# Halves of q made over 128 partitions and moved by DMA, in a pre-norm attention and mixture-of-experts layer

## The chip, the cores and the metric

The kernel runs on 1 core of one Trainium2 chip. The metric is the device time of one execution in microseconds; lower is better.

## The reference

The input x has 4 batches of 512 tokens of width 128. The layer adds an attention block, then a mixture of experts. Cut to what matters:

```python
def attention(x, ln1_g, ln1_b, Wq, Wkv, Wo, ln2_g, ln2_b):     # 16 heads of 64
    xn = layernorm(x, ln1_g, ln1_b)
    q = (xn @ Wq) * 64 ** -0.5                   # one q for each head
    k, v = split(xn @ Wkv)                       # one k and one v for all heads
    attn = softmax(einsum('bhid,bjd->bhij', q, k))
    out = einsum('bhij,bjd->bhid', attn, v)
    return layernorm(out @ Wo, ln2_g, ln2_b)

x = x + attention(layernorm(x), ...)
y = layernorm(x)
top 2 of 8 experts by softmax(y @ gate_w.T), weights scaled to sum 1
x = x + sum over the two of weight * (up * gelu(gate)) @ down
```

All is float32 in and out.

## The kernel before

**Precision.** TensorE multiplies float32 quickly in a format with a shorter mantissa. So q and k are kept as a high half (the value copied to that format) and a low half (the value less the high half). A head's q lies in `q_hl`: partitions 0 to 63 hold the high half, 64 to 127 the low half, so that one matmul over 128 partitions against `khh` (the high half of k, twice) adds high*high and low*high. `q_hm` holds the high half once more in partitions 0 to 63, and in partition 64 the negative row maximum of each query; a matmul with `kly` (low half of k and a row of ones) adds high*low and takes the maximum off. Both tensors have 10 slots, one for each head in turn.

**Steps.** `attention_schedule` makes one list of steps, sorted by a slot number and an order within it; every engine walks this list and does its part of each step, in that order. The unit is one score step: `EXP` n is at slot n, 256 in all (64 heads x 4 key tiles of 128), so 8 slots are a pair of heads and 64 slots a batch. What follows is measured in these slots.

- `Q` (line 1105 to 1107): TensorE makes q of a pair of heads in the bank `q_ps`, 128 partitions: 64 for each head.
- `QHI` (line 1077): ScalarE copies each head's 64 rows to the high half in `q_hl`, two instructions. `QLO` (line 1008): VectorE subtracts, two instructions, and writes partitions 64 to 127. GpSimd copies both high halves to `q_hm` (line 935).
- `MAX` (line 1170): TensorE computes high-part scores with queries on the partitions, 4 for each head; VectorE reduces them to row maxima (line 1019). Two buffers.
- `SHIFT` (line 1177): the maxima of four heads are turned; ScalarE writes them negated to `mrow` (line 1068); SP moves them by DMA to partition 64 of `q_hm` (line 871) and then issues four fills of the row lists in DRAM (line 877), as long as there are any.
- `EXP` (line 1199, 1201): the scores, keys on the partitions; ScalarE's exponential writes `prob` (line 1095).
- `PV` (line 1215): the product with v, TensorE. GpSimd adds up the probabilities (lines 950, 956). `SUM`, `RECIP`, `RSPLIT`, `NORM`, `OUT` normalize a unit of 8 heads and project them; `RSPLIT` writes `rhl` on VectorE (line 717), which `NORM`'s matmul (line 769) reads.
- Beside them run the layer norms, k and v of the next batch, and the routing of the batch before (`AFTER_STEPS`: `CHOOSE`, `RANK`, `PLACE` and so on, largely on VectorE; line 586 is the end of `CHOOSE5`; `RANK`'s matmuls are line 406 and behind), with GpSimd's indirect sends of rows (line 476).

The Q of pair k stands at slot 8k - 19 - lead (the lead is 6), the first MAX of the pair at 8k - 22, its first EXP at 8k. Pairs 0 to 3 have places of their own.

**The bank.** `q_ps` is shared by Q, k, v, the turned maxima and the routing: before TensorE writes it anew it waits for the reader of the last use (`bank_read`).

**SP.** The queue of DMAs that SP issues is in order. At step `V` of the last batch (slot 153) it issues the 8 loads of the experts' weights, 512 KB each (line 669), into `raw_w`, in front of the rows of `SHIFT` at slot 155, which TensorE waits for at slot 160.

Behind the attention a second block runs 39 tiles of 128 rows through the experts. SP loads each tile's rows; the last 22 are loaded into what was `psums`.

## Time and profile before

| | |
|---|---|
| median of 3 runs | 622.52 us (621.23 to 623.45) |
| span of the profiled execution | 619.0 us |
| TensorE busy | 576.5 us, 93% |
| VectorE busy | 419.2 us, 68% |
| GpSimd busy | 394.9 us, 64% |
| ScalarE busy | 303.0 us, 49% |
| DMA queue of SP | 24.50 MB, 12.1% of 16 engines' span |

The profile is of one execution. The span reaches from its first instruction to its last; the device time of a run has some microseconds around it, 3.5 by the median. The attention takes the span up to about 467 us, the experts the rest. An engine's share of busy time is an average over stages. The end of a matmul is modelled, so a busy TensorE can still wait inside a row; waits show as idle time in front of an instruction, with the instruction that ended it.

### The profile page before, as it was taken

To read this page: it belongs to the slowest core of one execution; us is meant where nothing else is said; L and a number is where in the kernel's file an instruction comes from. 1 tells how busy PE (TensorE), PEld (TensorE's weight loads), DVE (VectorE), ACT (ScalarE), POOL (GpSimd) and SP (SyncE) were. 2 spreads that over 40 slices of the span, in tenths; PEclk is the share of its full clock that TensorE was granted. 3 is DMA by queue.
4 is the path that set the end of the run, shared out by engine and by line. 5 is a ranking of instruction groups with operands and counts; after the bars stand their busy time and mean duration, and the time that the engine had idled before them with its cause. 6 is when DMAs were issued, how large, how long until landed. Compare 5 with 4: busy or idle time off the path is not lost. (4 is left out here: it accounts for less than half of the span.)

```text
span 619.0 us, 8823 instructions
## 1 busy us (share of the span) xinstructions
PE 576.5 (93%) x2611; PEld 328.8 (53%) x2611; DVE 419.2 (68%) x816; ACT 303.0 (49%) x568; POOL 394.9 (64%) x326
## 2 busy tenths in 40 slices
PE   8899999999999999989999988999998869999980
PEld 6455454454554454445544534444443558888870
DVE  4976659658747978875587789877487468444433
ACT  2345645355555554454656434455636453555530
POOL 5357667658668855698597558859746934454330
PEclk9999999999999999889999999999999999999995
DMA  6111011010101100070000000000006101230005
GB/s 177 69 70 70 25 48 69 1 69 6 65 28 43 71 1 2 4 272 32 2 0 2 1 2 18 18 1 1 9 2 191 46 22 32 66 92 27 26 11 203
DMA packets 23981, 29.29 MB, mean 47 GB/s; under 512 B 4403, under 2 KB 14901, under 8 KB 23936
## 3 DMA queue, kind: packets, MB, share of 16 engines
q1 hardware_dynamic: 21664, 24.50, 12.1%
q0 software_dynamic: 2272, 4.24, 2.0%
q8 instruction: 23, 0.38, 0.2%
q14 instruction: 22, 0.18, 0.1%
HBM read 13.73 MB, written 15.32 MB: 47 GB/s over the span
## 5 line engine op out<-in xcount | busy, mean ns | idle before, releaser
L1095 ACT ACTIVATE prob<-s_ps 128x512 f32<-128x512 f32 x256 | 150.5, 598 | 183.0 <-PE s_ps L1201 181.0
L1019 DVE TENSOR_REDUCE rowmax<-max_ps 128x1 f32<-128x512 f32 x256 | 173.1, 685 | 81.6 <-PE max_ps L1170 79.5
L950 POOL TENSOR_TENSOR fold<-prob 128x1024 f32<-128x1024 f32 x63 | 149.6, 2374 | 95.2 <-ACT prob L1095 94.7
L1215 PE MATMUL pv_ps<-prob,v 128*64 128x512 f32 x512 | 139.1, 623 | 0.0
L1199 PE MATMUL s_ps<-q_hl,khh 128*128 128x512 f32 x256 | 118.0, 461 | 0.6 <-ACT prob L1095 0.6
L1170 PE MATMUL max_ps<-khh,q_hl 128*128 128x512 f32 x256 | 103.6, 410 | 6.5 <-DVE q_hl L1008 3.3
L1201 PE MATMUL s_ps<-q_hm,kly 65*128 65x512 f32 x256 | 102.1, 399 | 0.0
L1199 PEld LDWEIGHTS s_ps<-q_hl,khh 128*128 128x128 f32 x256 | 48.6, 190 | 79.2 <-ACT prob L1095 59.8
L956 POOL TENSOR_TENSOR psums<-fold 128x512 f32<-128x512 f32 x63 | 81.7, 1296 | 4.9
L1170 PEld LDWEIGHTS max_ps<-khh,q_hl 128*128 128x128 f32 x256 | 49.1, 192 | 26.5 <-DVE rowmax L1019 9.4
L1201 PEld LDWEIGHTS s_ps<-q_hm,kly 65*128 65x128 f32 x256 | 48.8, 191 | 9.0 <-issue 3.4
L1215 PEld LDWEIGHTS pv_ps<-prob,v 128*64 128x64 f32 x512 | 25.7, 136 | 46.0 <-issue 35.1
L476 POOL DMA_INDIRECT sorted_rows<-xr,place_i x32 | 34.5, 1078 | 21.5 <-issue 12.2
L1008 DVE TENSOR_TENSOR q_hl<-q_ps,q_hl 64x512 fp32r<-64x512 f32 x64 | 44.1, 689 | 5.5 <-ACT q_hl L1077 4.2
L1550 PE MATMUL sum_ps<-wd,ht 128*128 x312 | 41.8, 277 | 6.0 <-DVE raw L1409 5.2
L1400 DVE TENSOR_TENSOR ha<-up_ps,gl 128x512 f32<-128x512 f32 x39 | 26.9, 691 | 29.5 <-PE up_ps L1528 22.8
L1550 PEld LDWEIGHTS sum_ps<-wd,ht 128*128 128x128 f32 x312 | 37.9, 192 | 7.4 <-issue 7.4
L1077 ACT ACTIVATE q_hl<-q_ps 64x512 fp32r<-64x512 f32 x64 | 37.6, 588 | 7.9 <-PE q_ps L1107 7.0
L1361 POOL DMA_INDIRECT parts<-raw,psums x22 | 21.3, 970 | 30.4 <-DVE raw L1409 27.6
L935 POOL TENSOR_SCALAR q_hm<-q_hl 64x1024 fp32r<-64x1024 f32 x32 | 33.3, 1040 | 6.7 <-ACT q_hl L1077 6.7
L727 DVE TENSOR_TENSOR ao<-sum_ps,raw 128x512 f32<-128x512 f32 x32 | 22.0, 689 | 21.6 <-PE sum_ps L769 21.3
L779 PE MATMUL y_ps<-ao,wof 128*128 128x512 f32 x64 | 34.8, 628 | 0.0
(227 smaller groups left out, 783.2 us busy)
## 6 DMA issues: line engine op xcount, KB each, us to landing
sorted_rows<-raw_w SPq DMA_DIRECT2D x36, 260.0 KB, 2.6
raw_w<-in_gate_upT SPq DMA_DIRECT2D x8, 512.0 KB, 7.5
wd<-in_downT SPq DMA_DIRECT2D x8, 256.0 KB, 3.6
raw_w<-parts SPq DMA_DIRECT2D x8, 256.0 KB, 4.6
psums<-sorted_rows SPq DMA_DIRECT2D x22, 65.0 KB, 1.8
x<-in_x SPq DMA_DIRECT2D x4, 256.0 KB, 5.8
out<-x SPq DMA_DIRECT2D x4, 256.0 KB, 2.5
xs_first<-sorted_rows SPq DMA_DIRECT2D x15, 65.0 KB, 2.2
```

The source lines that it names most:

```text
L779: nc.tensor.matmul(y_ps[:, :], wof[:, c, :], ao[:, k % 2, :], start=c == 0, stop=c == PAIRS - 1).then_inc(out_mm, 1)
L950: nc.gpsimd.tensor_tensor(fold[:, :, :], prob[:, head % 4, 0:2, :], prob[:, head % 4, 2:4, :], ALU.add).then_inc(prob_folded, 1)
L956: nc.gpsimd.tensor_tensor(psums[:, head % SUM_SLOTS, :], fold[:, 0, :], fold[:, 1, :], ALU.add).then_inc(head_sum, 1)
L1008: nc.vector.tensor_tensor(q_hl[DH:P, h % Q_SLOTS, :], q_ps[DH * hd:DH * hd + DH, :], q_hl[0:DH, h % Q_SLOTS, :].bitcast(F32), ALU.subtract ...
L1019: nc.vector.tensor_reduce(rowmax[:, group % 2, it, i:i + 1], max_ps[:, k % 2, :], AX_X, ALU.max).then_inc(max_done, 1)
L1077: nc.scalar.activation(q_hl[0:DH, (2 * k + hd) % Q_SLOTS, :], q_ps[DH * hd:DH * hd + DH, :], ACT.Copy).then_inc(q_hi, 1)
L1095: nc.scalar.activation(prob[:, head % 4, jt, :], s_ps[:, k % 2, :], ACT.Exp, scale=SCALE).then_inc(exp_done, 1)
L1170: nc.tensor.matmul(max_ps[:, k % 2, :], q_hl[:, k // JT % Q_SLOTS, it * P:(it + 1) * P], khh[:, b % 2, :], start=True, stop=True).then_inc ...
L1199: nc.tensor.matmul(s_ps[:, k % 2, :], khh[:, b % 2, keys], q_hl[:, slot, :], start=True, stop=False)
L1201: nc.tensor.matmul(s_ps[:, k % 2, :], kly[0:DH + 1, b % 2, keys], q_hm[0:DH + 1, slot, :], start=False, stop=True).then_inc(score_mm, 1)
L1215: last = nc.tensor.matmul(pv_ps[DH * hd:DH * hd + DH, :], v[:, b % 2, jt, :], prob[:, head % 4, jt, :], start=(jt == 0), stop=(jt == JT - 1))
L1550: last = nc.tensor.matmul(down_ps[:, :], ht[:, k % 2, c * P:(c + 1) * P], wd[:, weights(k, DN, c * P, P)], start=c == 0, stop=c == FC - 1)
```

## The change

For pairs 5 and up (`DIRECT = 5`), 27 of the 32:

- ScalarE makes the high halves of both heads by one instruction over 128 partitions into a new tile `qh`; VectorE the low halves by one into `ql`.
- A new step `QMOVE` on SP moves them by six DMAs of 64 partitions x 2 KB: the high half of each head to `q_hl`, the low half of each to `q_hl`, the high half of each to `q_hm`. GpSimd's copy is gone for these pairs. SP waits for `qh_made`, for the scores of the head that had the slot, and for `ql_made`.
- ScalarE and VectorE write `qh` and `ql` anew only when the moves of the pair before have landed. TensorE waits for the moves in place of the instructions.
- Q of these pairs stands at 8k - 27 - lead, 8 slots earlier; the Q of pair 5 at slot 13 (15 before).
- `mrow` has no tile of its own any more; it lies in partitions of `q_hm` that are otherwise unused. In the experts' block, the last 22 tiles share one semaphore for two loads each.

The diff, without the list of semaphore names:

```diff
@@ -61,11 +61,13 @@
     for pair in range(units * UP):
         u, p = divmod(pair, UP)
 
-        at = (-30, -11, *FIRST_Q_AT)[pair] if pair < 4 else 8 * pair - 19 - lead
+        at = (-30, -11, *FIRST_Q_AT)[pair] if pair < DIRECT + 1 else 8 * pair - 27 - lead
         place(at, 3, "Q", u, p)
         place(at + 1, 3, "QHI", u, p)
 
         place(-8 if pair == 1 else at + 1, 4, "QLO", u, p)
+        if pair >= DIRECT:
+            place(at + 1, 4.5, "QMOVE", u, p)
         for jt in range(JT):
             place(8 * pair + PV_AT[jt], 2, "PV", u, p * JT + jt)
         place(8 * pair + PV_AT[-1] + 1, 1, "RAW", u, p)
@@ -120,7 +122,9 @@
 LAST_STEPS = (("RECIP", 0), ("RECIP", 1), ("RECIP", 2), ("RECIP", 3), ("RSPLIT", 0), ("NORM", 0), ("NORM", 1), ("OUT", 0),
               ("NORM", 2), ("OUT", 1), ("NORM", 3), ("OUT", 2), ("OUT", 3))
 
-FIRST_Q_AT = (-3, 3)
+FIRST_Q_AT = (-3, 3, 7, 13)
+
+DIRECT = 5
 
 FIRST_SHIFT_AT = (-7.5, 2)
 
@@ -319,7 +323,15 @@
         tiles_ready = sem("tiles_ready")
         w_in = [sem(f"w_in{e}") for e in range(E)]
         down_mm = sem("down_mm")
-        xs_in = [sem(f"xs_in{k}") for k in range(NT)]
+        xs_in = [sem(f"xs_in{k}") for k in range(FIRST_TILES)] + [sem(f"xs_pair{n}") for n in range((REST + 1) // 2)]
+
+        def tile_in(k):
+
+            return k if k < FIRST_TILES else FIRST_TILES + (k - FIRST_TILES) // 2
+
+        def tiles_with(k):
+
+            return sum(tile_in(n) == tile_in(k) for n in range(NT))
         count = {"dve": 0, "pool": 0, "ln": 0, "ln_pool": 0, "ln_dve": 0}
 
         def link(dve, ins):
@@ -788,6 +800,8 @@
         with ExitStack() as att:
             q_hl = sb(att, "q_hl", [P, Q_SLOTS, S], F32R)
             q_hm = sb(att, "q_hm", [P, Q_SLOTS, S], F32R)
+            qh = sb(att, "qh", [P, S], F32R)
+            ql = sb(att, "ql", [P, S], F32R)
             xh = sb(att, "xh", [P, 2, S], F32R)
             xl = sb(att, "xl", [P, 2, S], F32R)
             wqh = sb(att, "wqh", [P, HEADS * DH], F32R)
@@ -805,7 +819,7 @@
             wvh = sb(att, "wvh", [P, DH], F32R)
             wvl = sb(att, "wvl", [P, DH], F32R)
             rowmax = sb(att, "rowmax", [P, 2, TPB, 4])
-            mrow = sb(att, "mrow", [4, 2, S], F32R)
+            mrow = q_hm[3 * P // 4:3 * P // 4 + 4, 0:2, :]
             prob = sb(att, "prob", [P, 4, JT, S])
             fold = sb(att, "fold", [P, 2, S])
 
@@ -824,6 +838,16 @@
 
             blank_set = sem("blank_set")
             mrow_in = [sem(f"mrow_in{n}") for n in range(2)]
+            q_in = sem("q_in")
+            qm_in = sem("qm_in")
+
+            def q_came(eng, k):
+
+                eng.wait_ge(q_in, 16 * 4 * (k - DIRECT + 1))
+
+            def q_top_came(eng, k):
+
+                eng.wait_ge(qm_in, 16 * 2 * (k - DIRECT + 1))
 
             def rows_came(eng, n):
 
@@ -859,6 +883,23 @@
                                  (gw[:, :], gate_wT), (tri[:, :, :], lower)):
                     sp.dma_start(dst, src).then_inc(consts2_in, 16)
                 for kind, u, a in steps:
+                    if kind == "QMOVE":
+                        k = u * UP + a
+                        parts_of = [slice(DH * hd, DH * hd + DH) for hd in range(2)]
+                        slots = [(2 * k + hd) % Q_SLOTS for hd in range(2)]
+                        sp.wait_ge(qh_made, k - DIRECT + 1)
+                        if 2 * k + 2 > Q_SLOTS:
+                            sp.wait_ge(score_mm, (2 * k + 2 - Q_SLOTS) * JT)
+                        for held, slot in zip(parts_of, slots):
+                            sp.dma_start(q_hl[0:DH, slot, :].bitcast(F32),
+                                         qh[held, :].bitcast(F32)).then_inc(q_in, 16)
+                        sp.wait_ge(ql_made, k - DIRECT + 1)
+                        for held, slot in zip(parts_of, slots):
+                            sp.dma_start(q_hl[DH:P, slot, :].bitcast(F32),
+                                         ql[held, :].bitcast(F32)).then_inc(q_in, 16)
+                        for held, slot in zip(parts_of, slots):
+                            sp.dma_start(q_hm[0:DH, slot, :].bitcast(F32),
+                                         qh[held, :].bitcast(F32)).then_inc(qm_in, 16)
                     if kind == "SHIFT":
                         head, heads = shift_heads[u]
 
@@ -927,7 +968,7 @@
                         for first, end in zip(WQ_PAIRS, WQ_PAIRS[1:]):
                             part = slice(first * P, end * P)
                             split(wq_raw[:, part], wqh[:, part], wql[:, part], wq_split)
-                    if kind == "Q":
+                    if kind == "Q" and u * UP + a < DIRECT:
                         k = u * UP + a
 
                         pool.wait_ge(q_hi, 2 * (k + 1))
@@ -1001,7 +1042,14 @@
                         nc.vector.tensor_tensor(kly[0:DH, b % 2, :], k_bank(b)[0:DH, :],
                                                 khh[0:DH, b % 2, :].bitcast(F32),
                                                 ALU.subtract).then_inc(kl_ready, 1)
-                    if kind == "QLO":
+                    if kind == "QLO" and u * UP + a >= DIRECT:
+                        k = u * UP + a
+                        dve.wait_ge(qh_made, k - DIRECT + 1)
+                        if k > DIRECT:
+                            q_came(dve, k - 1)
+                        nc.vector.tensor_tensor(ql[:, :], q_ps[:, :], qh[:, :].bitcast(F32),
+                                                ALU.subtract).then_inc(ql_made, 1)
+                    elif kind == "QLO":
                         for hd in range(2):
                             h = 2 * (u * UP + a) + hd
                             dve.wait_ge(q_hi, h + 1)
@@ -1067,12 +1115,16 @@
                             rows_came(act, u - 2)
                         nc.scalar.activation(mrow[0:heads, u % 2, :], shift_bank(u)[0:heads, :], ACT.Copy,
                                              scale=-1.0).then_inc(mrow_ready, 1)
-                    if kind == "QHI":
+                    if kind == "QHI" and u * UP + a >= DIRECT:
                         k = u * UP + a
                         act.wait_ge(q_mm, k + 1)
-                        if 2 * k >= Q_SLOTS:
-
-                            act.wait_ge(score_mm, (2 * k + 2 - Q_SLOTS) * JT)
+                        if k > DIRECT:
+                            q_came(act, k - 1)
+                            q_top_came(act, k - 1)
+                        nc.scalar.activation(qh[:, :], q_ps[:, :], ACT.Copy).then_inc(qh_made, 1)
+                    elif kind == "QHI":
+                        k = u * UP + a
+                        act.wait_ge(q_mm, k + 1)
                         for hd in range(2):
                             nc.scalar.activation(q_hl[0:DH, (2 * k + hd) % Q_SLOTS, :], q_ps[DH * hd:DH * hd + DH, :],
                                                  ACT.Copy).then_inc(q_hi, 1)
@@ -1111,7 +1163,8 @@
                     if kind in AFTER_STEPS:
                         return after_bank_read(kind, u)
                     return {"XT": (xnT_sb, u + 1), "K": (kl_ready, u + 1), "V": (v_ready, u + 1),
-                            "Q": (q_lo, 2 * (u * UP + a + 1)), "SHIFT": (mrow_ready, u + 1)}[kind]
+                            "Q": (q_lo, 2 * (u * UP + a + 1)) if u * UP + a < DIRECT else (ql_made, u * UP + a - DIRECT + 1),
+                            "SHIFT": (mrow_ready, u + 1)}[kind]
 
                 def keep_busy(times):
 
@@ -1160,8 +1213,10 @@
                     if kind == "MAX":
                         i, it = divmod(a, JT)
                         k = u * UH * JT + a
-                        if it == 0:
+                        if it == 0 and u * UH + i < 2 * DIRECT:
                             pe.wait_ge(q_lo, u * UH + i + 1)
+                        elif it == 0 and i % 2 == 0:
+                            q_came(pe, u * UP + i // 2)
                         if 2 <= k < 12:
                             keep_busy(BUSY["rows"])
                         if k >= 2:
@@ -1190,7 +1245,10 @@
                             n = first_heads.index(k // JT)
                             rows_came(pe, n)
                         if a % (2 * JT) == 0:
-                            pe.wait_ge(q_top, u * UP + i // 2 + 1)
+                            if u * UP + i // 2 < DIRECT:
+                                pe.wait_ge(q_top, u * UP + i // 2 + 1)
+                            else:
+                                q_top_came(pe, u * UP + i // 2)
                         if k >= 2:
 
                             pe.wait_ge(exp_done, k - 1)
@@ -1510,7 +1568,7 @@
                         pe.wait_ge(xeh_ready, k)
                     else:
                         pe.wait_ge(xel_ready, k - RAW_TILES)
-                    pe.wait_ge(xs_in[k], 16)
+                    pe.wait_ge(xs_in[tile_in(k)], 16 * tiles_with(k))
                     nc.tensor.transpose(xt_ps[:, :], rows(k)[:, 0:P], ident[:, :]).then_inc(xt_mm, 1)
 
                 def weights(k, of_each, first, width):
```

Where Q of pairs 5 and 6 goes on TensorE: the rows of slots 14 and 15, before and then after the change (`s_ps` are the two score matmuls of a slot, `max_ps` a MAX matmul).

```order
L1199 MATMUL s_ps<-q_hl,khh 128x512
L1201 MATMUL s_ps<-q_hm,kly 128x512
L1170 MATMUL max_ps<-khh,q_hl 128x512
L1215 MATMUL pv_ps<-prob,v 64x512 x2
L1199 MATMUL s_ps<-q_hl,khh 128x512
L1201 MATMUL s_ps<-q_hm,kly 128x512
L1170 MATMUL max_ps<-khh,q_hl 128x512
L1105 MATMUL q_ps<-xh,wqh 128x512
L1106 MATMUL q_ps<-xh,wql 128x512
L1107 MATMUL q_ps<-xl,wqh 128x512
```

```order
L1157 MATMUL q_ps<-xh,wqh 128x512
L1158 MATMUL q_ps<-xh,wql 128x512
L1159 MATMUL q_ps<-xl,wqh 128x512
L1257 MATMUL s_ps<-q_hl,khh 128x512
L1259 MATMUL s_ps<-q_hm,kly 128x512
L1225 MATMUL max_ps<-khh,q_hl 128x512
L1273 MATMUL pv_ps<-prob,v 64x512 x2
L1257 MATMUL s_ps<-q_hl,khh 128x512
L1259 MATMUL s_ps<-q_hm,kly 128x512
L1225 MATMUL max_ps<-khh,q_hl 128x512
L1157 MATMUL q_ps<-xh,wqh 128x512
L1158 MATMUL q_ps<-xh,wql 128x512
```

In both, the first score matmul shown is that of slot 14. Before, the first Q shown behind slot 15 is pair 5's; after, pair 5's stands in front of slot 14 and pair 6's is the one behind slot 15.

The same place on ScalarE, from the exponential of slot 13 on; `q_hl` rows are the two high halves of a pair, `qh` the new one. Before:

```order
L1095 ACTIVATE prob<-s_ps 128x512 x4
L1077 ACTIVATE q_hl<-q_ps 64x512 x2
L1095 ACTIVATE prob<-s_ps 128x512 x4
L737 ACTIVATE raw<-pv_ps 128x512
L1095 ACTIVATE prob<-s_ps 128x512 x2
L372 ACTIVATE x<-x,offset,rstd 128x128 x4
L1095 ACTIVATE prob<-s_ps 128x512 x2
L1077 ACTIVATE q_hl<-q_ps 64x512 x2
```

After:

```order
L1147 ACTIVATE prob<-s_ps 128x512 x2
L1124 ACTIVATE qh<-q_ps 128x512
L1147 ACTIVATE prob<-s_ps 128x512 x2
L1124 ACTIVATE qh<-q_ps 128x512
L1147 ACTIVATE prob<-s_ps 128x512 x4
L749 ACTIVATE raw<-pv_ps 128x512
L1147 ACTIVATE prob<-s_ps 128x512 x2
L384 ACTIVATE x<-x,offset,rstd 128x128 x4
```

Only two exponentials, those of slots 15 and 16, now stand between the high half of pair 5 and that of pair 6.

SP's queue around the loads of the weights, before: rows of the maxima (`mrow`), fills (`sorted_rows`), and the weight loads (`raw_w<-in_gate_upT`) behind the rows of slots 123 and 139.

```order
L871 DMA q_hm<-mrow 1x2x512 x2
L877 DMA sorted_rows<-raw_w 128x520 x4
L871 DMA q_hm<-mrow 1x2x512 x4
L669 DMA raw_w<-in_gate_upT 128x1024 x8
L871 DMA q_hm<-mrow 1x2x512 x12
```

After, from the moves of slot 152 on:

```order
L894 DMA q_hl<-qh 64x512 x2
L898 DMA q_hl<-ql 64x512 x2
L901 DMA q_hm<-qh 64x512 x2
L681 DMA raw_w<-in_gate_upT 128x1024 x8
L912 DMA q_hm<-q_hm 1x2x512 x2
L894 DMA q_hl<-qh 64x512 x2
```

The weight loads are issued behind the moves of slots 144 and 152, of which the second pair's wait for the Q of slot 151; the rows of slot 155 are still the next behind the loads.

## Rows read from the trace of the kernel before

**Rows 1.** The page: span, and TensorE's busy time, share and instructions.

```profile
span 619.0 us, 8823 instructions
PE 576.5 (93%) x2611; PEld 328.8 (53%) x2611; DVE 419.2 (68%) x816; ACT 303.0 (49%) x568; POOL 394.9 (64%) x326
```

**Rows 2.** The page's groups of instructions: count, busy us, mean ns, idle before.

```profile
L1095 ACT ACTIVATE prob<-s_ps 128x512 f32<-128x512 f32 x256 | 150.5, 598 | 183.0 <-PE s_ps L1201 181.0
...
L1008 DVE TENSOR_TENSOR q_hl<-q_ps,q_hl 64x512 fp32r<-64x512 f32 x64 | 44.1, 689 | 5.5 <-ACT q_hl L1077 4.2
...
L1400 DVE TENSOR_TENSOR ha<-up_ps,gl 128x512 f32<-128x512 f32 x39 | 26.9, 691 | 29.5 <-PE up_ps L1528 22.8
...
L1077 ACT ACTIVATE q_hl<-q_ps 64x512 fp32r<-64x512 f32 x64 | 37.6, 588 | 7.9 <-PE q_ps L1107 7.0
...
L935 POOL TENSOR_SCALAR q_hm<-q_hl 64x1024 fp32r<-64x1024 f32 x32 | 33.3, 1040 | 6.7 <-ACT q_hl L1077 6.7
```

**Rows 3.** Busy time, clock and DMA share in the stretch 78 to 450 us.

```profile
78.00:450.00 372.00, 362.68 (x1487) 178.64 (x1486) 272.89 (x484) 191.47 (x360) 269.98 (x196) 0.99 0.09 31
```

**Rows 4.** Line 1008, who waited for it: us in total, times.

```profile
  PE max_ps L1170: 3.3, 3
```

**Rows 5.** Timeline from 244 us: start, us, engine, line.

```profile
245.18 1.05 POOL L935 TENSOR_SCALAR q_hm<-q_hl 64x1024 fp32r<-64x1024 f32 x1
...
246.16 0.68 DVE L1019 TENSOR_REDUCE rowmax<-max_ps 128x1 f32<-128x512 f32 x1
246.87 1.41 DVE L1008 TENSOR_TENSOR q_hl<-q_ps,q_hl 64x512 fp32r<-64x512 f32 x2
...
247.61 0.75 PE L1170 MATMUL max_ps<-khh,q_hl 128*128 128x512 f32 x1 [1.56 <-DVE q_hl L1008]
...
249.79 1.71 PE L1215 MATMUL pv_ps<-prob,v 128*64 128x512 f32 x4
...
251.43 0.41 PE L406 MATMUL q_ps<-picked,before 128*128 128x32 f32 x2
```

**Rows 6.** Timeline from 360 us.

```profile
363.25 1.41 DVE L1008 TENSOR_TENSOR q_hl<-q_ps,q_hl 64x512 fp32r<-64x512 f32 x2
...
363.98 0.49 PE L1170 MATMUL max_ps<-khh,q_hl 128*128 128x512 f32 x1 [1.47 <-DVE q_hl L1008]
...
365.43 0.50 PE L1170 MATMUL max_ps<-khh,q_hl 128*128 128x512 f32 x1 [0.49 <-DVE rowmax L1019]
```

**Rows 7.** Two short stretches; the last three numbers are clock, DMA share, GB/s.

```profile
248.00:250.00 2.00, 2.00 (x6) 0.90 (x7) 1.68 (x4) 0.60 (x1) 0.07 (x1) 0.50 0.00 0
272.00:275.00 3.00, 3.00 (x8) 0.89 (x6) 1.88 (x4) 1.67 (x3) 2.68 (x3) 0.50 1.02 410
```

**Rows 8.** Timeline from 266 us.

```profile
270.05 0.50 PE L769 MATMUL sum_ps<-rhl,headsel 128*128 128x512 f32 x1 [2.10 <-DVE rhl L717]
```

**Rows 9.** Timeline: the first score matmul of slots 14 and 19.

```profile
50.92 0.41 PE L1199 MATMUL s_ps<-q_hl,khh 128*128 128x512 f32 x1
...
58.73 0.40 PE L1199 MATMUL s_ps<-q_hl,khh 128*128 128x512 f32 x1
```

**Rows 10.** The weight loads (line 669), then the timeline of slots 151 to 160.

```profile
L669 SPq DMA_DIRECT2D raw_w<-in_gate_upT x8: 424/432/710, 266.7 to 270.2; - x8
...
DMA to landing us min/median/max: 4.1/7.5/10.7
...
289.18 1.20 ACT L1077 ACTIVATE q_hl<-q_ps 64x512 fp32r<-64x512 f32 x2
...
298.90 1.19 SPq L871 DMA_DIRECT2D q_hm<-mrow  x2
...
304.09 0.40 PE L1199 MATMUL s_ps<-q_hl,khh 128*128 128x512 f32 x1
```

**Rows 11.** The page's DMA issues: count, KB each, median us to landing.

```profile
sorted_rows<-raw_w SPq DMA_DIRECT2D x36, 260.0 KB, 2.6
...
gw<-in_gate_wT SPq DMA_DIRECT2D x1, 4.0 KB, 4.4
```

6 lines of the change are left out of this document (3 added, 3 removed).

## Prediction

> **What bounds the kernel now.** I read the page first. TensorE is busy 93% of a span of 619.0 us [rows 1], and the change does not touch its work: the same 2003 rows of TensorE code are in both programs. So the change can only give back time in which TensorE waits, or take more. The table by stretches says how much there is. From 78 to 450 us, the steady part of the attention, TensorE is busy 362.68 of 372 us [rows 3]: at most 9.3 us are idle, and some of that belongs to waits the change does not touch. The totals on the page mislead here. ScalarE is busy half of the span, VectorE two thirds, and both wait for TensorE; taking work from an engine that waits gives nothing by itself.
>
> Then I asked who waits for the instruction that the change replaces, VectorE's low halves of q (line 1008). TensorE's MAX matmul waited for it 3 times, 3.3 us together [rows 4]. Two of these waits are long. I number the 256 score steps (EXP) as slots; a pair of heads is 8 slots.
>
> - At 247.61 a MAX matmul starts after 1.56 us idle [rows 5]. The reader is to see the row above it: VectorE came to the row maximum only at 246.16, behind the routing work of the batch before, and to the two q halves at 246.87. The MAX matmul stands for the first head of the pair whose halves are being made, so it waits for the first of them.
> - At 363.98 the same, 1.47 us, and at 365.43 another 0.49 us for the row maximum that the halves had delayed [rows 6]. This is the same place of the next batch.
>
> The first of these also costs clock: the granted clock is 0.50 in the stretch 248 to 250, that is 1.2 GHz instead of 2.4 [rows 7], after a gap of 1.56 us. The second gap, nearly as long, cost none.
>
> A third long wait, 2.10 us at 270.05, is for rhl [rows 8], not for q; it too is followed by a stretch at 0.50 [rows 7].
>
> **The change, part by part.** It holds for 27 of the 32 pairs.
>
> *ScalarE.* Two instructions of 588 ns become one over 128 partitions. The nearest row is the exponential of the same shape, 598 ns [rows 2]; so 27 x 0.58 = 15.7 us less. ScalarE waits for TensorE in this part, so: 0 on the path.
>
> *VectorE.* Two of 689 ns become one; VectorE's product of the same shape (line 1400) takes 691 ns [rows 2]. 27 x 0.69 = 18.6 us less. Where VectorE is behind, this matters; I count it inside the two places below and nowhere else.
>
> *GpSimd.* 27 copies of 1040 ns go away [rows 2], 28 us. GpSimd waits for ScalarE's probabilities in most of this time: 0. One of these copies, at 245.18 to 246.23, lies in front of the late row maximum at 246.16 [rows 5]; it may give up to 0.5 us there, which I don't count.
>
> *The longer lead.* From pair 6 on, Q stands 8 slots earlier, exactly one pair. So in the steady state each slot has the same instructions as before, made for the next pair. The first MAX of a pair comes 11 slots behind its Q instead of 3. The MAX matmul of 247.61 could start where TensorE went idle, 247.61 - 1.56 = 246.05. The next MAX then needs the row maximum that ends at 246.84, about 0.2 us of wait, and the PV group that started at 249.79 starts at about 247.2; the matmuls at 251.43 come at 248.2 [rows 5]: 3.2 us, of which about half is clock. At 363.98 the same working gives: MAX at 363.98 - 1.47 = 362.5, the next one at 363.3 (limited by the row maximum right ahead of the halves, which start at 363.25), so 365.43 becomes 363.3: 2.1 us [rows 6]. The third wait on q is the rest, under 0.3 us, and lies in the first pairs, which are unchanged. Sum of the gains: 5.3 us. Bounds: below, the 3.0 us of the two idle times alone; above, 3.2 + 2.1 plus 2 us if the lighter VectorE also shortens the wait at 270.05.
>
> *The moves.* Six DMAs a pair, 128 KB each, 162 in all. Issue: SP's DMAs of the maxima rows take 0.60 us each, the weight loads 0.50 [rows 10], so 3.0 to 3.6 us a pair. Landing: the 260 KB fills take 2.6 us [rows 11], an upper bound for half the bytes. At the 410 GB/s of [rows 7] 260 KB are 0.6 us of it; 2.0 stay as the way in and out, the lower bound, and with 0.3 for 128 KB I take 2.3. So a pair's q is in place about 6 us behind its high half, and the MAX that reads it comes 10 slots, some 17 us, later: hidden in the steady state. The DMA engines are busy 0.09 of this stretch [rows 3] and take 768 KB more each 13.9 us (slots 14 to 160 take 304.09 - 50.92 us [rows 9, 10], 1.73 a slot). If that cover were gone, each pair would wait up to 4 us.
>
> *The start.* Pair 5's Q goes to slot 13 and pair 6's to slot 15, two slots apart. Pair 6's high half on ScalarE waits until all moves of pair 5 have landed. Slot 14 starts at 50.92 [rows 9]; Q of pair 5 now stands in front of it and takes 0.7. High half done about 53.4, low half 54.4, last move issued at 56.0 to 56.4, landed at 58.3 to 58.8. Pair 6's high half is then done at 58.8 to 59.4 and the exponential of slot 17 behind it at 59.4 to 60.0. TensorE's slot 19, at 58.73 before [rows 9], would come at 59.7 (0.7 for the second Q, 0.3 for the bank) and needs that exponential: a wait of 0 to 0.4. With the bank and the row maximum queued behind the low half on VectorE I take 0.6 us lost; bounds 0.3, and 2.5 if the moves take twice as long. The 0.7 of the earlier Q comes back at the end.
>
> *The weight loads.* SP's queue is in order, and this is the one place that it is pushed. The 8 loads of the experts' weights were issued from 266.7, behind the rows of slot 139 [rows 10]. They stand at slot 153 in SP's list, and until now nothing held SP. Now the moves of slots 144 and 152 stand in front, and those of 152 wait for the low half of the Q of slot 151. That Q's high halves start at 289.18 [rows 10]; with one instruction the high half is done at 289.8, the low at 290.5, six issues end at about 293.1, and the loads follow, 26 us later than before. They took 270.2 + 10.7 - 266.7 = 14.2 us from first issue to last landing, with GpSimd's own sends between them; the 4.19 MB alone at the 410 GB/s of [rows 7] take 10.2, and with 2.0 for the way in and out 12.2. So they end at 305.3 (bounds 304.6 and 307.4). Behind them in the queue come the maxima rows of the next four heads, issued at 298.90, which TensorE needs at 304.09 [rows 10]. A DMA of 4 KB behind a full queue does wait: gw took 4.4 us to land behind the x loads [rows 11]. The rows so land at about 305.5: 1.4 us of wait, bounds 0.6 and 3.4. The clock decides what such a wait is worth beyond itself; I take nothing for it here and price it in rival 2.
>
> No row here shows a transfer over 64 partitions. The Trainium skill (SBUF — State Buffer, "Door 1: The DMA port swizzle") says that partitions 0 to 63 reach 8 of 16 ports, with 218 GB/s as the limit. By it, an estimate, a move takes 0.6 us of transfer instead of the 0.3 that 410 GB/s gives, the last moves reach 0.6 us further into the weight loads, and the sum would be 0.6 us higher. The sum goes by the rows.
>
> *The end.* Tiles from 17 on wait for two row loads instead of one. They run some tiles ahead of TensorE: 0.
>
> **Sum.** -5.3 + 0.6 + 1.4 = -3.3 us; the profile's 619.0 becomes 615.7. Around the span lie 622.52 - 619.0 = 3.5 us. Some of the 2 us of VectorE's relief and of the 0.5 us that GpSimd's missing copy may give are likely, so I forecast -3.7: 618.8 us. A difference under 0.3%, 1.9 us, can't be told from none.
>
> **Rivals.**
> 1. *The rows come in time.* If the loads end by 304, or the rows' two packets don't wait for the whole queue, only the start costs: -5.3 + 0.6 = -4.7, with the other relief up to -6.5: 616.0 to 617.8. Against it speaks the landing of gw. 0.15.
> 2. *The gain is eaten.* A gap of 1.56 us cost clock and one of 1.47 did not [rows 5 to 7]; the wait behind the weights is about as long. With it some 1.6 us more; and if the late row maxima take the place of the wait for q (DVE stays behind by the routing work), the gain falls to 3.0. Then -3.0 + 0.6 + 1.4 + 1.6 = +0.6, or with one of the two -1.7: 620.8 to 623.1, no change. 0.22.
> 3. *Slower: rows behind the weights.* The loads end at 307.4 or later because moves and loads share the engines; TensorE waits 3.4 us or more, falls to 1.2 GHz for 2 us, and the probabilities of the head behind come late: 6 or more against 5.3, with the start at its 2.5. +2.5 to +4: 625 to 626.5. It decides once wait and clock together pass 6.6 us (5.3 + 1.9 - 0.6). 0.13.
> 4. *The change does nothing*: the two waits stay, since they were VectorE's lateness. Against it, MAX at 247.61 starts at once with the end of the first q half, 0.74 us into the pair, and not with the row maximum. With it nothing is gained and the losses of 2.0 stay: 624.5; 0.02, counted in rival 3.
>
> My forecast, -1.9 to -5.0, has 0.50. Faster than 0.3%: 0.50 + 0.15 = 0.65; same 0.22; slower 0.13. The range leaves out the far part of rival 3 and little else: 615.0 to 623.3; the likeliest case alone holds 617.5 to 620.6.
>
> **What would show it.** Right: no wait of MAX for q at about 244 and 358; the granted clock 1.00 where it was 0.50 at 248; ScalarE idle some 2 us or more at about 56 for a DMA; a wait of TensorE for a DMA in front of the score matmul of slot 160, near 300 in the new span, with the weight loads issued at about 290; one VectorE operation of about 690 ns per pair. Wrong: that last wait missing or over 3 us, MAX waiting for the row maximum at the two places, or moves that take over 4 us to land.

## The result, and the profile after

The changed kernel takes 625.38 us (median; 622.66 to 628.13), the kernel before on the same chip 622.28 us (617.94 to 626.67). The ratio is 1.006, 95% interval 1.0036 to 1.0083: slower, by more than 0.3%. I had forecast 618.8 us and given this side 0.13. Measured again, the same kernel gave 1.0074 (below). Ratios, here and below, are of fast runs alone (a few slow or stray ones are left out of them), and so they are not quite the quotients of the medians.

The page of the changed kernel, top and groups:

```profile
span 625.0 us, 8929 instructions
...
PE 580.8 (93%) x2611; PEld 331.1 (53%) x2611; DVE 398.8 (64%) x789; ACT 288.3 (46%) x541; POOL 367.7 (59%) x299
...
L1257 PE MATMUL s_ps<-q_hl,khh 128*128 128x512 f32 x256 | 118.7, 464 | 3.7 <-DMA q_hm<-q_hm 2.1
L1225 PE MATMUL max_ps<-khh,q_hl 128*128 128x512 f32 x256 | 103.8, 411 | 5.8 <-DVE rowmax L1067 4.3
...
q_hm<-qh SPq DMA_DIRECT2D x54, 128.0 KB, 2.3
```

VectorE, ScalarE and GpSimd have 20, 15 and 27 us less to do than in [rows 1], as they should, and a move lands in 2.3 us, as forecast. None of this bounds the kernel. The span is 6.0 us longer all the same, and TensorE is busy 4.3 us more (576.5 in [rows 1]) with the same 2611 matmuls: a good part of the loss is not idle time but matmuls at the lower clock. The lines to read are still the idle times of TensorE, since the clock falls behind them: the score matmul of line 1257 waited 2.1 us for a DMA, and MAX (line 1225) 4.3 us for row maxima.

The two profiles are not equally lucky. In every run on record the device time is 1.7 to 2.1 us above the run's span, and not the 3.5 us that I had put there. So the profile before, of 619.0 us, is of an execution of about 620.8 us (an estimate from these), about 1.5 under the median of 622.28. That of the changed kernel took 626.78 us, 1.4 over its median. About half of the 6.0 us is this choice.

To find the places I took from both traces the start of the first score matmul of every pair (of 8 slots), and of tiles of the experts' block, and subtracted. Pairs are counted from 0; "again" is experiment 11, "four edits" experiment 12, and the last column experiment 9. Each number is what is lost (+) or won (-) between one mark and the next, in us, profile against profile:

```
                               changed kernel     four edits    kernel before, list step
                               first   again      to it         one slot earlier
pair 0 -> 1                     +0.03   +0.16     -1.42          -0.18
pair 1 -> 3 (Q of 5 and 6)      +2.22   +2.17     +0.66           0.00
pair 3 -> 16                    +0.01    0.00      0.00          -0.01
pair 16 -> 19                   -2.15   -3.76     -3.76          -1.52
pair 19 -> 21 (slot 160)        +2.37   +4.83      0.00           0.00
pair 24 -> 26                   -2.63   -2.66     -2.68          +4.47
pair 26 -> 27                   +3.85   +5.32     -0.02           0.00
pair 27 -> 28 (Q of 5 returned) -1.00   -1.01     -1.00          -0.01
tile 0 -> 8                     +2.34   +1.26     +1.39          +2.18
tile 17 -> 20                   +0.83   +0.71      0.00          +0.03
```

The -1.42 at pair 0 -> 1 is no gain of the edits: the kernel of experiment 3 has it too, with a granted clock of 1.00 from 12 to 50 us where the kernel before has 0.96. Tile 8 -> 17 was 0.2 us longer in the first column and 2.0, 2.0 and 2.7 us in the others; everything else is under 0.9 us. Three of my steps are seen at their places: the start, slot 160, and the two late row-maximum places (pairs 16 and 24). Two losses I had not priced: pair 26, and tile 17.

**The start.** Timeline of the changed kernel, from the first to the second new Q:

```profile
52.26 0.59 ACT L1124 ACTIVATE qh<-q_ps 128x512 fp32r<-128x512 f32 x1
...
55.55 1.24 SPq L901 DMA_DIRECT2D q_hm<-qh  x2
...
58.89 0.60 ACT L1124 ACTIVATE qh<-q_ps 128x512 fp32r<-128x512 f32 x1 [3.09 <-DMA q_hm<-qh]
59.39 1.08 ACT L1147 ACTIVATE prob<-s_ps 128x512 f32<-128x512 f32 x2
...
59.52 0.69 DVE L1050 TENSOR_TENSOR ql<-q_ps,qh 128x512 fp32r<-128x512 f32 x1 [3.39 <-ACT qh L1124]
60.03 0.50 PE L1257 MATMUL s_ps<-q_hl,khh 128*128 128x512 f32 x1 [0.82 <-ACT prob L1147]
```

The second `qh` waits 3.09 us for the moves of the first. Behind it stands an exponential, and TensorE waits 0.82 us for that, so slot 19 starts at 60.03 (58.73 in [rows 9]). A MAX matmul behind it waits 0.54 us more for the row maximum that VectorE makes behind the late low half.

**Slot 160.** The weight loads, the rows of the maxima behind them, and the score matmul that needs these:

```profile
L681 SPq DMA_DIRECT2D raw_w<-in_gate_upT x8: 432/446/592, 293.1 to 296.7; - x8
...
DMA to landing us min/median/max: 3.6/6.9/9.7
...
298.52 1.29 SPq L912 DMA_DIRECT2D q_hm<-q_hm  x2
...
305.99 0.50 PE L1257 MATMUL s_ps<-q_hl,khh 128*128 128x512 f32 x1 [2.11 <-DMA q_hm<-q_hm]
```

The last load lands at 296.7 + 9.7 = 306.4. The rows, issued 1.8 us behind it, come only near the end of this stretch: TensorE is idle for 2.11 us, until 305.99.

**Pairs 16 and 24.** Where [rows 5] have two low halves in 1.41 us and MAX waiting 1.56 us for them, there is now:

```profile
247.34 0.68 DVE L1067 TENSOR_REDUCE rowmax<-max_ps 128x1 f32<-128x512 f32 x1
...
247.94 0.68 DVE L1050 TENSOR_TENSOR ql<-q_ps,qh 128x512 fp32r<-128x512 f32 x1
...
248.17 0.47 PE L1225 MATMUL max_ps<-khh,q_hl 128*128 128x512 f32 x1 [0.33 <-DMA q_hl<-qh]
...
249.27 0.50 PE L1225 MATMUL max_ps<-khh,q_hl 128*128 128x512 f32 x1 [0.18 <-DVE rowmax L1067]
```

The DMA that the first wait names belongs to the next pair; what ended here is the row maximum, at 248.02. The granted clock stays at 1.00, where [rows 7] have 0.50. At pair 24 it is the same with 0.27 and 0.18 us (1.47 and 0.49 in [rows 6]), and a part of the gain lies one pair further on, at a matmul that waits for `rhl`. First before, then after:

```profile
385.21 0.50 PE L769 MATMUL sum_ps<-rhl,headsel 128*128 128x512 f32 x1 [1.61 <-DVE rhl L717]
```

```profile
384.58 0.50 PE L781 MATMUL sum_ps<-rhl,headsel 128*128 128x512 f32 x1 [0.37 <-DVE rhl L729]
```

The wait of 2.10 us in [rows 8], for the same product, did not get shorter: it is 2.30 us.

**Pair 26**, the place that I had not looked at. First the kernel before, then the changed one, VectorE and GpSimd only:

```profile
391.03 1.05 POOL L935 TENSOR_SCALAR q_hm<-q_hl 64x1024 fp32r<-64x1024 f32 x1
...
392.25 1.07 POOL L476 DMA_INDIRECT sorted_rows<-xr,place_i  x1 [0.17 <-issue]
...
393.31 0.17 DVE L628 TENSOR_SCALAR taken<-more_upto 128x8 f32<-128x8 f32 x1
...
394.59 2.42 POOL L950 TENSOR_TENSOR fold<-prob 128x1024 f32<-128x1024 f32 x1
```

```profile
391.89 0.97 POOL L488 DMA_INDIRECT sorted_rows<-xr,place_i  x1 [0.30 <-issue]
...
392.69 2.62 DVE L640 TENSOR_SCALAR taken<-more_upto 128x8 f32<-128x8 f32 x1
392.87 2.39 POOL L991 TENSOR_TENSOR fold<-prob 128x1024 f32<-128x1024 f32 x1
...
395.34 1.29 POOL L997 TENSOR_TENSOR psums<-fold 128x512 f32<-128x512 f32 x1
395.54 1.12 DVE L643 TENSOR_TENSOR more_upto<-more_upto,more 128x8 f32<-128x8 f32 x1
396.69 0.69 DVE L1067 TENSOR_REDUCE rowmax<-max_ps 128x1 f32<-128x512 f32 x1
...
397.44 0.80 PE L1225 MATMUL max_ps<-khh,q_hl 128*128 128x512 f32 x1 [2.04 <-DVE rowmax L1067]
```

Line 628 is now line 640: an operation on 128x8 elements of the routing's list step. It took 0.17 us, and takes 2.62, ending when GpSimd's `fold` beside it ends. Before, the fold started 1.28 us behind this operation, and now 0.18 us; the difference is the copy of 1.05 us that stood in GpSimd's queue in front of two sends and the fold, with nothing between them but the sends' issue (0.17 and 0.30 us). The row maximum queued behind it comes late, MAX waits 2.04 us, and the granted clock falls to 0.50 in 398 to 400.

### The profile page after: what moved, and what is told of

Read it like the earlier page. It is cut to its first block and busy times, and to the rows that moved or that the text cites. A ratio compares the mean times of both kernels' runs of the same rounds, so it can differ in the third digit from the quotient of the medians.

```text
span 625.0 us, 8929 instructions
## 1 busy us (share of the span) xinstructions
PE 580.8 (93%) x2611; PEld 331.1 (53%) x2611; DVE 398.8 (64%) x789; ACT 288.3 (46%) x541; POOL 367.7 (59%) x299
## 5 line engine op out<-in xcount | busy, mean ns | idle before, releaser
L1528 ACT ACTIVATE ht<-q_ps 128x512 f32<-128x512 f32 x39 | 23.3, 597 | 24.5 <-PE q_ps L1595 22.9
L1520 ACT ACTIVATE gl<-gate_ps 128x512 f32<-128x512 f32 x39 | 23.3, 598 | 19.1 <-PE gate_ps L1586 16.1
L720 DVE RECIPROCAL rinv<-sum_ps 128x128 f32<-128x128 f32 x32 | 29.9, 941 | 2.6 <-PEq L800 2.6
```

The costliest lines, as they stand in the source:

```text
L720: last = nc.vector.reciprocal(rinv[:, quarter], sum_ps[:, quarter])
```

## Experiments

All were timed beside the kernel before, whose median was 622.54 us beside 1 to 4, 620.57 beside 5 to 8 and 624.12 beside 9 to 12, each time on another chip. So kernels of different groups are compared by their ratios, and not by their medians. Ratios are to the kernel before, with the 95% interval.

**1. Weight loads first.** SP issues the eight loads right behind the maxima rows of slot 139, ahead of the moves of slots 144 and 152, and not at step `V`:

```diff
+                        if u == 10:
+                            sp.wait_ge(rows_filled, 16 * FILLS)
+                            for e in range(E):
+                                load_gate_up(sp, e)
-                    if kind == "V" and u == NB - 1:
-                        sp.wait_ge(rows_filled, 16 * FILLS)
-                        for e in range(E):
-                            load_gate_up(sp, e)
```

> The changed kernel with one part undone: SP issues the 8 weight loads where the kernel before did, right behind the rows of slot 139, ahead of the moves of slots 144 and 152. Theory (rows behind the weights): the wait of the score matmul of slot 160 for a DMA, 2.3 us in the changed kernel's profile, goes, pair 19 takes 16.1 us again instead of 18.3, and the time is some 2.3 us less than the changed kernel's 625.4. Rival (the queue only shifts the wait): the weights now delay the moves of slot 144, and the time stays within 1 us of 625.4.

622.18 us, ratio 1.0019 (0.9991 to 1.0047), span 620.2. The loads are issued from 265.4, the wait at slot 160 is gone (0.00 at pair 19 -> 20, +2.27 with the change alone). So this loss was the order in SP's queue. The ratio fell by 0.4%, about what I had expected (2.3 us).

**2. Q of pair 6 three slots later.** Slot 18 and not 15 (the condition that picks `FIRST_Q_AT` takes in one pair more, not shown):

```diff
-FIRST_Q_AT = (-3, 3, 7, 13)
+FIRST_Q_AT = (-3, 3, 7, 13, 18)
```

> The changed kernel with pair 6's Q at slot 18 in place of slot 15, so that Q of pairs 5, 6 and 7 stand 5 slots apart. Theory (ScalarE waits for the round trip of pair 5's moves): ScalarE's idle 3.1 us for a DMA in front of the second high half goes, and pairs 1 and 2 together lose their 1.5 us; the time is 1.5 us less than 625.4. Rival (the loss of pairs 1 and 2 is the extra Q in this stretch alone): nothing changes.

624.55 us, ratio 1.0031 (0.9995 to 1.0067). Pair 1 -> 3 costs 0.62 and not 2.22: the extra Q alone is left, 1.6 us are saved. In this profile the second high half no longer waits:

```profile
59.21 0.59 ACT L1124 ACTIVATE qh<-q_ps 128x512 fp32r<-128x512 f32 x1
...
59.83 0.69 DVE L1050 TENSOR_TENSOR ql<-q_ps,qh 128x512 fp32r<-128x512 f32 x1 [0.19 <-ACT qh L1124]
```

**3. The lead alone**, in the kernel before, without single instructions or moves:

```diff
-        at = (-30, -11, *FIRST_Q_AT)[pair] if pair < 4 else 8 * pair - 19 - lead
+        at = (-30, -11, *FIRST_Q_AT)[pair] if pair < 6 else 8 * pair - 27 - lead
-FIRST_Q_AT = (-3, 3)
+FIRST_Q_AT = (-3, 3, 7, 13)
```

> The kernel before with one part of the change alone: Q of pairs 5 and up 8 slots earlier, still with two instructions per half and GpSimd's copy, no moves. Theory (the lead is what gives time back, the moves only cost): both waits of MAX for q go, 2.5 us at pair 16 and about 2 at pairs 24 and 25, no wait at slot 160, no start loss: 617 to 619 us, some 4 us less than the kernel before. Rival (the lighter VectorE and GpSimd gave the gain): MAX waits for the row maximum at the same places and the time is within 1.5 us of 622.3.

626.44 us, ratio 1.0079 (1.0049 to 1.0109): slower. The wait for q is gone and two waits for row maxima stand in its place:

```profile
246.31 0.68 DVE L1019 TENSOR_REDUCE rowmax<-max_ps 128x1 f32<-128x512 f32 x1
247.01 1.41 DVE L1008 TENSOR_TENSOR q_hl<-q_ps,q_hl 64x512 fp32r<-64x512 f32 x2
247.13 0.47 PE L1170 MATMUL max_ps<-khh,q_hl 128*128 128x512 f32 x1 [0.91 <-DVE rowmax L1019]
...
249.20 0.80 PE L1170 MATMUL max_ps<-khh,q_hl 128*128 128x512 f32 x1 [1.13 <-DVE rowmax L1019]
```

My expectation of 617 to 619 us failed, and the gain that I put down to the lead is not the lead's. MAX waits 0.91 + 1.13 us here, about as much as the kernel before waits in the execution of experiment 4 (1.57 + 0.33), and at both places the two profiles lose the same against the profile before: 1.80 us at pair 16 -> 19 and 3.1 at pair 24 -> 26. In the times all twelve runs lie at 624.6 or above, while the kernel before reaches down to 618.0. It also loses at the start: pair 1 -> 3 costs 1.63 us without a single move, 0.69 of it a wait of TensorE for the bank, and 0.71 comes back at pair 27 -> 28.

In the changed kernel the two waits at pair 16 are 0.33 and 0.18 us. Experiment 8 tells which part of the change took away which.

**4. Row pairs alone.** The kernel before with one semaphore for the loads of two tiles, as in the diff.

> The kernel before with the semaphores of the last 22 row loads shared by two, as in the changed kernel, and nothing else. Theory (the first of these tiles waits for the second load and TensorE's sequencer gets to the next tile late): 0.8 to 1.1 us more than the kernel before, with TensorE idle about 0.5 to 0.8 us in front of the first gate matmul behind the turn of tile 17. Rival (the loads are ahead): no difference, and the 0.8 us in the changed kernel's profile come from elsewhere.

624.02 us, ratio 1.0018 (0.9979 to 1.0056). The time tells nothing; the profile has +0.89 at tile 17 -> 20, the same loss as in the changed kernel. Its attention is that of the kernel before, and yet it has +3.38 at pair 16 -> 17 and +3.15 at pair 24 -> 25 against the profile before. This is the clock. The rows below give the stretch and its length, then busy time and instructions of TensorE, its weight loads, VectorE, ScalarE and GpSimd, then granted clock, DMA share and GB/s. First the kernel before, then this one, in the stretches behind the wait for q:

```profile
250.00:252.00 2.00, 2.00 (x9) 0.66 (x8) 0.59 (x1) 0.00 (x0) 2.00 (x1) 0.72 0.00 0
252.00:254.00 2.00, 2.00 (x15) 1.09 (x14) 1.11 (x2) 1.35 (x3) 1.57 (x2) 1.00 0.00 0
```

```profile
250.00:252.00 2.00, 2.00 (x5) 0.39 (x6) 0.69 (x1) 0.00 (x0) 1.94 (x1) 0.50 0.00 0
...
254.00:256.00 2.00, 2.00 (x8) 0.90 (x11) 1.04 (x2) 1.63 (x3) 0.00 (x0) 0.50 0.00 0
256.00:258.00 2.00, 2.00 (x9) 0.50 (x2) 1.90 (x12) 0.00 (x0) 0.31 (x2) 0.50 0.00 0
```

The same matmuls after the same wait: the clock is back at 1.00 behind 252 in one execution and still at 0.50 in 256 to 258 in the other. So one profile of the kernel before is no fair base for the gain. Pair 16 -> 19 is 1.80 later here, and against this execution the change wins 3.9 to 5.6 us there instead of 2.2 to 3.8.

**5. Three repairs.** The changed kernel with 1 and 2 and a semaphore of its own for tile 17 (`tile_in` is shifted by one to fit, not shown):

```diff
-        xs_in = [sem(f"xs_in{k}") for k in range(FIRST_TILES)] + [sem(f"xs_pair{n}") for n in range((REST + 1) // 2)]
+        xs_in = [sem(f"xs_in{k}") for k in range(FIRST_TILES + 1)] + [sem(f"xs_pair{n}") for n in range(REST // 2)]
```

> The changed kernel with three parts undone at once: the weight loads back behind the rows of slot 139, pair 6's Q at slot 18, and the load of tile 17 on a semaphore of its own. Theory (the three losses are separate and add up): -2.3 or more at slot 160, -1.5 at pairs 1 and 2, -0.8 at tile 17, so 4 to 5 us less than the changed kernel's 625.4: about 621. The loss at pair 26 stays. Rival (they only moved the phase of the clock): the sum is under 3 us and other stretches give it back.

619.37 us, ratio 0.9984 (0.9951 to 1.0016), span 616.4: no difference to the kernel before that can be told. Slot 160 and tile 17 -> 20 are at 0.00, pair 26 -> 27 at +4.37, as expected.

**6. The list step one slot earlier.** The changed kernel with this alone:

```diff
-AFTER_AT = (29, 30, 33, 43, 51, 52, 54, 54, 55, 57, 58, 60, 63, 67, 69, 82, 84, 86, 88)
+AFTER_AT = (29, 30, 33, 43, 51, 52, 54, 54, 55, 57, 58, 60, 63, 67, 69, 81, 84, 86, 88)
```

> The changed kernel with VectorE's first list step of the batch (LIST0) one slot earlier, nothing else. In the changed kernel one VectorE instruction of this step, over 8 elements a partition, takes 2.62 us at 392.7 because GpSimd's send and its fold stand in the way, and MAX then waits 2.04 us for the row maximum, pair 26 taking 17.4 us instead of 13.6. Theory (a collision of VectorE with GpSimd that GpSimd's missing copy moved here): with the step elsewhere the 2.6 us instruction is short or costs under 1 us, and the time is 2 to 4 us less than 625.4. Rival (VectorE is simply behind here): the wait stays.

620.93 us, ratio 0.9989 (0.995 to 1.0028). Pair 26 -> 27 goes from +3.85 to -0.02. The operation takes its short time again, well ahead of the fold:

```profile
390.80 0.99 POOL L488 DMA_INDIRECT sorted_rows<-xr,place_i  x1 [0.15 <-POOL psums L997]
391.02 0.17 DVE L640 TENSOR_SCALAR taken<-more_upto 128x8 f32<-128x8 f32 x1
...
393.08 2.40 POOL L991 TENSOR_TENSOR fold<-prob 128x1024 f32<-128x1024 f32 x1
```

The operation lies inside one of GpSimd's sends here and is not held up, so a send alone does not hold it. In the changed kernel it started 0.17 us before a send ended and lasted through the fold.

**7. All four**, 5 and 6 together.

> The three parts of a_three and the earlier list step together. Theory: the four add up to 6 to 8 us less than the changed kernel: 617 to 619 us, below both kernels. Rival: phase effects of the clock eat half of it, 620 to 622.

615.21 us (613.33 to 617.17), ratio 0.9898 (0.9862 to 0.9934), span 611.9. Faster than both kernels, by more than I had expected (617 to 619; the kernel before was 1.7 us faster on this chip than beside the change).

**8. GpSimd's copy again.** The changed kernel with four moves; GpSimd copies the high halves to `q_hm` at the place that it had before. The two central lines of the edit (its waits and conditions are left out):

```diff
-                        for held, slot in zip(parts_of, slots):
-                            sp.dma_start(q_hm[0:DH, slot, :].bitcast(F32),
-                                         qh[held, :].bitcast(F32)).then_inc(qm_in, 16)
+                        nc.gpsimd.tensor_scalar(q_hm[0:DH, slots, :], q_hl[0:DH, slots, :].bitcast(F32),
+                                                1.0, 1.0, ALU.mult, ALU.mult).then_inc(q_top, 1)
```

> The changed kernel with one part undone: GpSimd again copies the high halves to q_hm, 1.04 us a pair in the place where it stood before (for the pair before, whose halves have landed), and four moves in place of six. Theory (GpSimd's copy set the phase of its fold against VectorE's list step): the loss of 3.9 us at pair 26 goes, and the weight loads are issued some 1.2 us earlier so that the wait at slot 160 falls from 2.3 to about 1 us; the gain at pairs 16 and 24 shrinks by up to 1 us, since VectorE again waits for this copy at the end of the routing. About 621 us. Rival (the fold's place comes from the lead or from TensorE): pair 26 still takes over 17 us.

620.4 us, ratio 0.9985 (0.9951 to 1.002), span 621.4. Pair 26 -> 27 is at 0.00, and the operation at 0.17 us:

```profile
391.75 1.05 POOL L972 TENSOR_SCALAR q_hm<-q_hl 64x1024 fp32r<-64x1024 f32 x1
...
394.03 0.17 DVE L640 TENSOR_SCALAR taken<-more_upto 128x8 f32<-128x8 f32 x1
...
395.32 2.42 POOL L994 TENSOR_TENSOR fold<-prob 128x1024 f32<-128x1024 f32 x1
```

With the copy pair 24 -> 26 gives -0.97 and not -2.63: there the missing copy was worth 1.7 us, of which 1.1 is the wait for `rhl`, 1.45 us here and 0.37 in the changed kernel. At pair 16 the waits of MAX are these:

```profile
247.43 0.47 PE L1227 MATMUL max_ps<-khh,q_hl 128*128 128x512 f32 x1 [0.94 <-DVE rowmax L1070]
...
248.53 0.50 PE L1227 MATMUL max_ps<-khh,q_hl 128*128 128x512 f32 x1 [0.17 <-DVE rowmax L1070]
```

The second is 0.17 us, as in the changed kernel, and 1.13 with the lead alone (3): that is what the single low half gives. The first is 0.94, as with the lead alone, and 0.33 in the changed kernel: that is the missing copy, 0.6 us. Pair 16 -> 17 gives -1.91 with the copy and -2.46 to -2.50 in the eight other profiles with the moves and the long lead.

At the start pair 1 -> 3 costs 1.02 and not 2.22, since two moves fewer stand in front of the second high half. Two expectations failed: the wait at slot 160 fell to 1.90 us only and not to about 1, and at pair 24 the gain shrank by more than 1 us.

**9. The list step in the kernel before.** The edit of 6, alone.

> The kernel before, with the list step at slot 81 instead of 82 and nothing else. My theory (the list step only undoes a loss that the change itself makes, since the kernel before has no such loss: its 128x8 operation took 0.17 us): within 1 us of the kernel before, 619.5 to 621.5, and the start of pair 27 within 0.5 us of it. Rival (the new place is better for any kernel, so the gain of the four edits together is not the change's): 2 us or more below the kernel before.

626.6 us beside 624.12 of the kernel before, ratio 0.9999 (0.9955 to 1.0043): no difference. Pair 26 -> 27 is at 0.00. At pair 16 this execution is the best of the kernel before: after waits of 1.53 and 0.49 us the clock stays at 1.00, and pair 16 -> 17 is 0.96 us shorter than in the profile before. My expectation for the position of pair 27 failed (+2.66), through the clock again; pair 24 -> 25 has +4.46 with the waits of [rows 6], the same to 0.01 us:

```profile
362.17 0.50 PE L1170 MATMUL max_ps<-khh,q_hl 128*128 128x512 f32 x1 [1.47 <-DVE q_hl L1008]
...
363.62 0.80 PE L1170 MATMUL max_ps<-khh,q_hl 128*128 128x512 f32 x1 [0.49 <-DVE rowmax L1019]
```

The busy times and the clock behind them (columns as above), first the kernel before, then this one:

```profile
366.00:368.00 2.00, 2.00 (x12) 1.15 (x11) 0.66 (x1) 0.00 (x0) 2.00 (x1) 1.00 0.00 0
```

```profile
366.00:368.00 2.00, 2.00 (x9) 1.75 (x8) 0.00 (x0) 0.00 (x0) 1.61 (x3) 0.50 0.00 0
...
370.00:372.00 2.00, 2.00 (x10) 0.20 (x8) 1.40 (x5) 0.60 (x1) 0.00 (x0) 0.50 0.00 0
```

**10. The change with the old lead.**

```diff
-        at = (-30, -11, *FIRST_Q_AT)[pair] if pair < DIRECT + 1 else 8 * pair - 27 - lead
+        at = (-30, -11, *FIRST_Q_AT)[pair] if pair < DIRECT + 1 else 8 * pair - 19 - lead
-FIRST_Q_AT = (-3, 3, 7, 13)
+FIRST_Q_AT = (-3, 3, 7, 15)
```

> The changed kernel with the lead taken back: Q of pair k at slot 8k - 19 - lead, pair 5 at slot 15, as before the change. The first MAX of a pair then stands 3 slots, 5.2 us, behind its Q; the last low half landed some 6.8 us behind the start of Q in the profile after (Q 50.9, moves of the low halves issued to 55.5, about 2.2 us more to land). My theory (the moves need the lead as cover): 1.6 us or more lost in each of 26 pairs, some of it again as clock: 655, between 640 and 670. Rival (the moves hide behind the other matmuls of these slots anyway, and the lead was not needed): under 630.

673.72 us, ratio 1.0785 (1.073 to 1.084). The page's group of MAX:

```profile
L1225 PE MATMUL max_ps<-khh,q_hl 128*128 128x512 f32 x256 | 106.8, 423 | 37.5 <-DMA q_hl<-ql 33.3
```

33.3 us of waits for the moves in 23 places: 17 of 1.3 to 1.6 us, two of 3.6 and 3.7, four small ones. The mean granted clock falls from 0.981 to 0.960. This is more than I had set (640 to 670). The longer lead gives no time of its own (3), but the moves can't be had without it.

**11 and 12. The change, and the change with all four edits, once more**, beside 9 and 10.

> The changed kernel once more, on the same chip as the others of this call: 5 us above the kernel before in the profile, 2 to 5 us in the times. If it comes out equal to the kernel before, the difference of the first measurement was the chip's and not the kernel's.

> The changed kernel with all four edits, once more: 4 to 7 us below the kernel before, 8 to 12 below the changed kernel. Rival (the first measurement of it was a lucky phase of the clock): within 2 us of the kernel before.

629.31 us, ratio 1.0074 (1.0039 to 1.011), and 616.4 us, ratio 0.986 (0.9815 to 0.9905), with 624.12 for the kernel before. Both results stand. The table above has both profiles. The profile of the changed kernel is 8.2 us above that of the kernel before and not 5, with 3.2 us at pair 19 -> 20 and 5.3 at pair 26 -> 27.

## Why the prediction was wrong

**The gain: size near, in part by luck, and reason half right.** I forecast 5.3 us at the two places, 3.2 and 2.1, and 0.4 for relief; the profile has 2.15 and 2.63. Of the 2.63, 1.2 come from the wait for `rhl` at 385, which I had not priced. And I put the gain down to the longer lead and counted the 18.6 us of VectorE and the 28 us of GpSimd at little or nothing. The lead alone made the kernel slower (3). The gain needs the single low half between the row maxima (0.68 us for 1.41) and the missing copy (8), which is worth 0.6 us at pair 16, where I had written of up to 0.5 and not counted it, and 1.7 at pair 24. "If the late row maxima take the place of the wait for q" was my rival 2, and it is what the lead alone does. At pair 24 -> 26 the gain is larger against other executions of the kernel before (4, 9), up to 7 us, since the change takes away a wait behind which the clock stayed low for 9 to 10 us in them. At pair 16 -> 19 it is 1.8 us larger against one and 1.5 smaller against the other. I read one execution and took its price for the price.

**The start: mechanism right, mis-sized.** The forecast times hold to 0.1 us (last move landed at 58.79, forecast 58.3 to 58.8; second high half done at 59.49, forecast 58.8 to 59.4). Net 1.2 us instead of 0.6: 2.22 at its place, 1.00 back at pair 27 -> 28. The two waits of TensorE were 0.82 and 0.54 us, where I had 0 to 0.4 for the first and named the row maximum behind the low half without a size. It was inside the bounds of 0.3 to 2.5. Experiment 2 removed 1.6, and 8 removed 1.2 by two moves fewer.

**The weight loads: right, 1.4 us forecast and 2.27 measured.** Loads issued at 293.15 (forecast 293.1), last landed at 306.4 (305.3); experiment 1 showed the cause. In four of the five profiles that have this wait and the long lead (2, 6, 8, 11) the following pair lost another 1.65 us to the clock, and in 11 the wait itself cost 0.9 more. I had it at nothing.

**GpSimd at 0: this step failed most.** "GpSimd waits for ScalarE's probabilities in most of this time: 0." True for the time of GpSimd and false for its position. The copy had been a spacer; without it the fold meets the list step, and 3.85 to 5.77 us go at pair 26: in the changed kernel 2.04 of it is the wait of MAX, the rest mostly clock. Experiments 6 and 8 show it from two sides, moving the one and putting back the other, and 9 shows that the kernel before had nothing to mend there. That the two collide over a shared resource is how the Trainium skill (SBUF — State Buffer, "Who interferes with whom") has it: a VectorE operation in a two-port mode, or with two inputs in SBUF, contends with a GpSimd operation that reads SBUF, and in a two-port mode one holds the shared ports for its whole instruction while the other is blocked. The trace agrees in the length: 2.62 us ends 0.05 us behind the fold, and 1.12 us of line 643 ends 0.03 us behind the `psums` addition. It doesn't show the port itself. The record of the operation starts 0.18 us before that of the fold, and yet it is the one that got long. I named this page in the prediction for the DMA ports, and not for this.

**Tiles from 17 on at 0: failed, 0.8 us.** Tile 17 is the first of its pair and its second load lands 1.1 us later than its own, 0.3 us before the matmul that turns its rows. The loads do run ahead, but not by enough at the turn to the second kind of tiles. That the shared semaphore is the cause is shown by 4 and 5. The profile has the idle time (0.54 us) in front of the next gate matmul, and doesn't show how it comes about.

**The sum by the profile**: start +1.2, slot 160 +2.4, pair 26 +3.9, tile 17 +0.8, against -2.15 and -2.63: +3.5. The medians say +3.1. The profile's own 6.0 has 2.3 more from tile 0 -> 8; eleven of the twelve experiments, of the kernel before too, have 1.0 to 2.2 there, so that is again the good profile of before and not the change. The forecast sum was -3.7: of the error of 7.2 us, 4.7 are the two steps at 0 and 1.6 the two that were mis-sized (0.6 and 1.0); the other 0.9 is the relief of 0.4 that I added and a gain 0.5 smaller.

**The rivals.** The time lies where rival 3 put it, but its mechanism (3.4 us or more at slot 160) was not what decided; no rival had the right one. That the time fell where this rival had it is chance. One of my signs of being wrong did come, MAX waiting for the row maximum at the two places, but with 0.5 us in each it left the gain standing.

## What to carry to other kernels

Removing work from an engine that waits moves what stands behind it. Look at what each removed instruction kept apart, VectorE against GpSimd above all, at every place of the program and not only where TensorE waits now. Before putting DMAs into an ordered queue, list what stands behind them; here a hoist of the large loads, two shifted steps and one more semaphore turned 3 to 5 us lost into 5 to 8 won, by the medians. Before pricing a wait from one profile, look at a second execution of the same kernel.
